# Moving the work at the seams of a two-layer kernel, and the first projection of each attention round

## The reference

```
xn = layernorm(x); s = L0_attn(xn); g = silu(L0_ffn(xn)); x = x + s * g
xn = layernorm(x); s = L1_attn(xn); g = silu(L1_ffn(xn)); x = x + s * g

L0_attn: gates f, i, o, z = xn W + b; c[t] = f c[t-1] + i z; out = o * tanh(layernorm(c))
L0_ffn:  4 trees of depth 5: each node's logits decide the child; the rows of the
         nodes on the path are gathered and summed: gelu(logits) * W_out
L1_attn: q, k, v = silu(conv4(xn W)), a gated delta rule over the 256 steps
         (16 heads of 8), out = rmsnorm(o) * silu(xn Wg) Wo
L1_ffn:  2 layers on 2 x 1024 tokens of 8 heads of 64:
         h = shift(x); q, k = rotary(l2norm(h wqkv)); x = x + softmax over a window of
         64 (own and previous block) @ wo; h = layernorm(shift(x)) * lng + lnb
         a, g = split(h w1 + b1); x = x + (a * gelu(g)) w2 + b2
```

## Time and profile before

| | |
|---|---|
| median of 3 executions | 1556.36 us (1556.31 to 1559.45) |
| the profiled execution | 1542.85 us, of it 1541.0 us span from first to last instruction |
| busy | PE 1294.8 us, DVE 1270.8, ACT 1228.2, POOL 945.8 |
| mean granted clock of TensorE | 0.938 of full |

### The profile page before, as it was taken

One profiled execution on the slowest core, in us unless ns is written; L12 is line 12 of the kernel. 1 busy time (PEld: TensorE's weight loads), 2 busy tenths in 40 slices (PEclk: granted clock), 3 DMA queues, 4 the chain that ended last, 5 costly groups with the idle time before them and its releaser, 6 DMA issues.

```text
span 1541.0 us, 31140 instructions
## 1 busy us (share of the span) xinstructions
PE 1294.8 (84%) x9368; PEld 881.3 (57%) x9368; DVE 1270.8 (82%) x4138; ACT 1228.2 (80%) x3366; POOL 945.8 (61%) x1472
## 2 busy tenths in 40 slices
PE   6987878888787665897589999999999999999986
PEld 3655656656566442343256666666666666666665
DVE  3278898978889896388499999999999999999985
ACT  2267887979787885677388998998989999989985
POOL 0237455464655641078587877878778778778752
PEclk9899999899999777898799999999999999999998
DMA  4359687696867875379301110111101111101243
GB/s 112 116 190 333 220 288 251 211 324 210 294 236 258 309 274 181 107 226 307 136 22 44 34 30 25 44 44 36 43 12 45 44 44 34 39 16 44 68 106 101
DMA packets 152407, 210.31 MB, mean 136 GB/s; under 512 B 68272, under 2 KB 105520, under 8 KB 152112
## 3 DMA queue, kind: packets, MB, share of 16 engines
q0 software_dynamic: 36864, 134.76, 25.0%
q1 hardware_dynamic: 114944, 71.98, 16.9%
q10 hardware_dynamic: 432, 1.59, 0.3%
HBM read 168.97 MB, written 26.74 MB: 127 GB/s over the span
## 4 chain that ended last, share of the span: by engine, by line
PE 26%; ACT 17%; issue 6%; DVE 2%; POOL 1%; ACTq 0%; DVEq 0%; POOLq 0%
ACT lo_s_ps L1756 5%; PE lo_qk_ps L1468 4%; PE lo_h_ps L1572 4%; PE lo_s_ps L1524 3%; PE lo_o_ps L1562 3%; ACT L1845 2%; ACT prepared_then_rounds L1816 2%; PE lo_ft_ps L1544 2%; ACT prepared_then_rounds L1770 2%; ACT lo_sq L1738 2%; PE lo_v_ps L1474 2%; PE lo_h_ps L1582 1%; PE lo_s_ps L1511 1%; ACT prepared_then_rounds L1764 1%; PE lo_o_ps L1496 1%
## 5 line engine op out<-in xcount | busy, mean ns | idle before, releaser
L341 POOL DMA_INDIRECT wide<-in_table,l_idx x128 | 129.6, 1012 | 204.2 <-DVE l_idx L810 128.7
L1756 ACT ACTIVATE lo_s_ps<-lo_s_ps,lo_nmx,lo_rn 128x128 f32<-128x128 f32 x504 | 219.5, 440 | 2.0 <-DVE lo_nmx L2073 1.6
L341 POOL DMA_INDIRECT l_rows<-in_table,l_idx x128 | 126.8, 990 | 81.9 <-DVE l_idx L817 45.7
L768 DVE CUSTOM_DVE_ANT_0 wide<-wide,xn_tok 128x128 f32<-128x128 f32 x512 | 155.9, 368 | 6.5 <-DMA wide<-in_table,l_idx 5.0
L1948 POOL TENSOR_TENSOR lo_de_kS<-lo_de_S,lo_de_ops 128x384 f32<-128x384 f32 x128 | 154.6, 1208 | 10.0
L651 ACT ACTIVATE l_rows<-l_rows,l_act 128x128 f32<-128x128 f32 x512 | 153.1, 387 | 1.0
L651 ACT ACTIVATE wide<-wide,l_act 128x128 f32<-128x128 f32 x512 | 153.1, 387 | 1.0
L768 DVE CUSTOM_DVE_ANT_0 l_rows<-l_rows,xn_tok 128x128 f32<-128x128 f32 x512 | 145.1, 347 | 7.6 <-DMA l_rows<-in_table,l_idx 7.6
L446 PE MATMUL l_S<-pre,l_AT 128*128 128x144 f32 (+3 forms) x832 | 129.3, 306 | 21.6 <-ACT l_AT L642 19.7
L446 PEld LDWEIGHTS l_S<-pre,l_AT 128*128 128x128 f32 (+2 forms) x832 | 116.2, 206 | 52.1 <-ACT l_AT L642 36.4
L1468 PE MATMUL lo_qk_ps<-wide,lo_hT 128*128 128x512 f32 x256 | 127.4, 621 | 18.6 <-DVE lo_c L2065 12.3
(11 more groups left out here) (321 smaller groups left out, 3655.0 us busy)
## 6 DMA issues: line engine op xcount, KB each, us to landing
lo_VE<-lo_V SPq DMA_DIRECT2D x64, 128.0 KB, 3.0
scratch_ops<-prepared_then_rounds SPq DMA_DIRECT2D x4, 1792.0 KB, 7.3
lo_de_ops<-scratch_ops SPq DMA_DIRECT2D x16, 448.0 KB, 4.2
scratch_qo<-prepared_then_rounds SPq DMA_DIRECT2D x8, 512.0 KB, 8.6
lo_de_qo<-scratch_qo SPq DMA_DIRECT2D x16, 256.0 KB, 4.6
x_tok<-in_x SPq DMA_DIRECT2D x8, 256.0 KB, 5.2
wide<-in_table,l_idx POOLq DMA_INDIRECT x128
l_rows<-in_table,l_idx POOLq DMA_INDIRECT x128
```

The costliest lines, as they stand in the source:

```text
L341: pool.indirect_dma_start(rows[L][:, r % SLOTS, p, :], None, a[f"table{L}"], bass.IndirectOffsetOnAxis(ap=at[:, p:p + 1], axis=0)).then_in ...
L768: ins = dve.tensor_tensor_reduce(z, z, x, 1.0, bias, ALU.mult, ALU.add, accum_out=pick[L][:, r % 2, k:k + 1])
L1756: ins = act.activation(here, here, ACT.Exp, scale=rn[:, v % 2, j, 2 * k + e:2 * k + e + 1], bias=nmx[:, j, e, k:k + 1], accum_out=sums[:, ...
```

## The change

Eight edits:

1. In `layer0_phase`, the load of the weights also waits for the last rows of level 5.
2. The bias product moves from the end of `prepare_phase` to the end of `layer0_phase`: TensorE does it ahead of `turn_m` of the last group, where it waits for the weights; VectorE's addition comes last in the phase. `b1` now lies in `wide`.
3. At the end of `prepare_phase`, the last two stores of gates and the store of the last answers are issued by ScalarE instead of SyncE.
4. The clearing of a column of `hT` moves from the start of `local_phase` to the start of `prepare_phase`.
5. In `local_phase`, TensorE waits for the constants only at its first `center`.
6. The projection of unit 0's second half goes to `s_ps` instead of `qk_ps`, so that it doesn't wait for the rotation of the first half.
7. In each round, `project(t, 0)` goes ahead of `turn_qk(t-1, 0, 0)` and `contract(t-3)`. The orders of VectorE, ScalarE and GpSimd in the rounds stay.
8. At the end, VectorE does the last unit's two products first, then those of part 7; SyncE's last stores follow, nine transfers in all instead of ten.

```diff
@@ layer0_phase, sync
             sp.wait_ge(spread[4].sem, spread[4].after(NT - 1))
+            sp.wait_ge(got[5][(NT - 1) % SLOTS].sem, got[5][(NT - 1) % SLOTS].after((NT - 1) // SLOTS))
             for k in WEIGHTS:
@@ layer0_phase, tensor
+            def bias():
+                pe.wait_ge(weights_in, 16 * len(WEIGHTS))
+                pe.wait_ge(acc_read.sem, acc_read.after(NG - 2))
+                for L_ in range(LAYERS):
+                    for side in (0, 1):
+                        for k, (at, wd) in enumerate(HCH):
+                            c, n = COLS["lnb1"] + L_, 6 * L_ + 3 * side + k
+                            ins = pe.matmul(acc[NG % 2][0:wd, 0, n:n + 1], m["w1"][:, L_, side * HID + at:side * HID + at + wd],
+                                            m["cols"][:, c:c + 1], start=True, stop=True)
+                ins.then_inc(multiplied.sem, 1)
...
+                if g == NG + 4:
+                    bias()
                 if on(g - 5):
                     turn_m(g - 5)
@@ prepare_phase, sync
-            keep(T // CT - 1)
-            for g in range(NG - 2, NG):
-                keep_gate(g)
+            keep(T // CT - 1, False)
@@ prepare_phase, scalar
+            for g in range(NG - 2, NG):
+                keep_gate(g)
+            keep_answers(T // CT - 1)
@@ local_phase
+        qk_of = lambda u, i: s_ps if (u, i) == (0, 1) else qk_ps
@@ local_phase, sync
             sp.wait_ge(last_ready.sem, last_ready.after(0))
+            sp.dma_start(rows(out)[:, NT - 2:NT, :], y_last[:, :, 3, :]).then_inc(y_stored.sem, 16)
+            sp.wait_ge(last_ready.sem, last_ready.after(1))
+            for h in (0, 1):
+                sp.dma_start(rows(out)[:, NT - 8 + h:NT - 2:2, :], y_last[:, h, 0:3, :]).then_inc(y_stored.sem, 16)
+            sp.wait_ge(last_ready.sem, last_ready.after(2))
             sp.dma_start(rows(out)[:, tiles(7), :], by_tile(u_buf(7))).then_inc(y_stored.sem, 16)
@@ local_phase, tensor
-            pe.wait_ge(consts.sem, 1)
             def project(u, i):
...
-                if n:
-                    pe.wait_ge(parts.sem, n)
+                if n >= 2:
+                    pe.wait_ge(parts.sem, n if n > 2 else 1)
...
                 if on(t - 2):
                     weigh(t - 2, 0)
+                if on(t):
+                    project(t, 0)
                 if on(t - 1):
                     turn_qk(t - 1, 0, 0)
                 if on(t - 3):
                     contract(t - 3)
-                if on(t):
-                    project(t, 0)
                 if on(t - 1):
                     turn_qk(t - 1, 0, 1)
@@ local_phase, vector, the end
             output(LAST)
-            multiply(7)
-            add_x(7)
             multiply_last(0, 3, 4)
-            add_last(0, 3, 1)
             multiply_last(3, 4, 5)
             add_last(3, 4, 2)
+            multiply(7)
+            add_last(0, 3, 2)
+            add_x(7)
```

More of the change, by code:

```diff
@@ L251, in layer0_phase @@
         scaling, scaled_rows = st("norm_scaling"), st("norm_rows")
+        multiplied = st("bias_multiplied")
         norm_rounds = [r for r in range(NG + 4) if 0 <= r < NG or 0 <= r - 4 < NG]
@@ L915, in _ @@
                     norms(g)
+            dve.wait_ge(multiplied.sem, 1)
+            for wd, ks in ((P, (0, 1)), (HCH[2][1], (2,))):
+                chunks = lambda ap: ap.rearrange("p (a k) -> p a k", k=3)[0:wd, :, ks[0]:ks[-1] + 1]
+                dve.tensor_tensor(chunks(m["b1"]), chunks(acc[NG % 2][:, 0, 0:6 * LAYERS]),
+                                  chunks(m["cols"][:, COLS["b1"]:COLS["b1"] + 6 * LAYERS]), ALU.add)
 def sized(ap):
@@ L997, in get, with keep @@
                 sp.dma_start(Y[x][:, n % 2].rearrange("p d t -> p (d t)"), scr[x][n].rearrange("b (h d) t -> (b h) (d t)", d=HD)).then_inc(y_in[x][n % 2].sem, 16)
-            def keep(c):
+            def keep(c, both=True):
                 sp.wait_ge(dve_done.sem, dve_done.after(2 * c + 1))
@@ L1004, in keep @@
                 sp.dma_start(rows, ops[:, c % 2].rearrange("p (s n) x -> p s (n x)", n=CB // 2)).then_inc(kept[c % 2].sem, 16)
-                for k, z in enumerate((qt, ow)):
+                for k, z in enumerate((qt, ow) if both else (qt,)):
                     sp.dma_start(scr["qo"][c, :, k], z[:, c % 2].rearrange("p n i g d -> p (n i g d)")).then_inc(kept[c % 2].sem, 16)
@@ L1053, in _ @@
                 pe.matmul(bank[g % 3][:], m["WgT"][:], m["xT_pad"][:, g * SG:(g + 1) * SG, TAPS - 1:], start=True, stop=True).then_inc(gated.sem, 1)
[L1054 to L1062, removed]
         @block.scalar
@@ L1107, in silu_gate, with keep_gate, keep_answers @@
                 act.activation(gate_buf[g], bank[g % 3][:], ACT.Silu).then_inc(gate_silued.sem, 1)
+            def keep_gate(g):
+                act.wait_ge(gate_silued.sem, gate_silued.after(g))
+                act.dma_start(scr["gate"][2 * g:2 * g + 2].rearrange("b r t -> r b t"), gate_buf[g].rearrange("p (b t) -> p b t", t=T)).then_inc(gate_stored.sem, 16)
+            def keep_answers(c):
+                act.wait_ge(pool_done.sem, pool_done.after(2 * c + 1))
+                act.dma_start(scr["qo"][c, :, 1], ow[:, c % 2].rearrange("p n i g d -> p (n i g d)")).then_inc(kept[c % 2].sem, 16)
             act.preload_act_table_set("natural_log_exp_and_others")
@@ L1266, in _ @@
                 dve.wait_ge(dve_done.sem, dve_done.after(n))
[L1267 to L1271, removed]
 def load_chunk(sp, m, scr, c):
@@ L1449, in _ @@
             sp.wait_ge(last_ready.sem, last_ready.after(0))
-            sp.dma_start(rows(out)[:, tiles(7), :], by_tile(u_buf(7))).then_inc(y_stored.sem, 16)
[L1451 to L1455, removed]
+            sp.dma_start(rows(out)[:, NT - 2:NT, :], y_last[:, :, 3, :]).then_inc(y_stored.sem, 16)
[3 more added lines that the diff above has]
+            sp.wait_ge(last_ready.sem, last_ready.after(2))
+            sp.dma_start(rows(out)[:, tiles(7), :], by_tile(u_buf(7))).then_inc(y_stored.sem, 16)
+            sp.wait_ge(y_stored.sem, y_stored.after(8))
         @block.tensor
         def _(pe):
-            pe.wait_ge(consts.sem, 1)
             def project(u, i):
@@ L1502, in scores @@
                 pe.wait_ge(k_kept.sem, k_kept.after(v, j + 1))
+                if (v, j) == (0, 0):
+                    pe.wait_ge(parts.sem, parts.after(0))
                 if (v, j) == (LAST, 1):
```

24 lines of the change are left out of this document (12 added, 12 removed).

## The result

The changed kernel takes 1660.01 us (median of 4 executions, 1655.09 to 1669.65), the kernel before on the same chip 1557.9: a ratio of **1.066 (1.0604 to 1.0715)**, +102 us. The forecast was +78 and the upper end of the range 1658. The direction and the mechanism were as predicted; the rounds cost 21 us more than in the sum. Of the kernels further down, one execution of turn_first took 2432 us where its other three took 1631 to 1638, and it stays out of the comparisons.

A forecast was written before the change was run, and what follows sets the result against it. Rounds, with TensorE and VectorE both over 92% busy, were taken as the bound. Stall +72.5 and clock +19, less 13.9 at the seams, gave +77.6 on 1556.36: 1634 us, range 1602 to 1658.

The forecast's parts named there:

- the mechanism: In the rounds: the contraction behind the projection makes VectorE's output 3.51 us late, delaying probabilities and TensorE's later steps.
- the size of the stall: In each round, TensorE's path from the second turn of q on runs 2.5 us late; 29 rounds make +72.5 us.
- The clock term: In the rounds, new TensorE idle time drops the clock in half of them, 1.3 us each: +19 us.
- The first rival: In the rounds: the same stall but the clock stays up, +58.6 us, 1615 us in all; chance 0.37.
- The second rival: In the rounds: projection 0.74 us earlier shortens each, 21.5 us gained, 1521 us in all; chance 0.03.
- The third: Rival: something else takes up the 3.5 us, rounds stay and only the seams count, 1542 us; chance 0.02.
- The fourth: Rival at layer 0's end: late weights make the bias product hold back the last group, 1642 us; chance 0.06.
- First layer: End of layer 0, edits 1 and 2: level 5's last rows arrive sooner, bias product fits idle time, -6.5 us.
- Preparation: End of preparation, edits 3 to 5: stores moved off SyncE give -2.1 us, first projection's wait for clearings gone -0.5.
- First unit: Edit 6: second projection in its own bank follows at once, GpSimd's wait shrinks, -3.3 us.
- The end: Edit 8: VectorE multiplies the last unit's product while waiting for the last mix, and fewer last stores, -1.5 us.

The follow-up runs named there:

- turn_first: The changed kernel with TensorE's order weigh, turn, project, contract, so only the contraction is behind the projection: ratio 1.0791, 120 us over the kernel before.
- order_only: The kernel before with edit 7 alone: ratio 1.0767, 117 us over the kernel before.
- output_late: The changed kernel with VectorE taking both answers and the first normalise ahead of output: ratio 1.0067, 10 us over the kernel before.
- contract_first: The changed kernel with TensorE's order weigh, contract, project, turn: ratio 1.0046, 6 us over the kernel before.
- scale_early: The changed kernel with GpSimd scaling k before the fourth step of the delta rule in a round: ratio 1.0637, 98 us over the kernel before.
- fill4: The changed kernel plus four unread matmuls a round in TensorE's idle time ahead of the turn of probabilities: ratio 1.0533, 80 us over the kernel before.
- seams_only: The changed kernel with edit 7 alone undone, the seven seam edits kept: ratio 0.993, 12 us under the kernel before.
- seams_early_w: The kernel with the seam edits alone, without edit 1's added wait for the weights' load: ratio 0.996, 6 us under the kernel before.

## Why the prediction was right and wrong

**The mechanism was right, and it is shown.** The changed kernel loses in the rounds alone (order_only), through VectorE's wait for the late contraction (output_late, contract_first), and the signs that the prediction named for the rounds are in the trace: the projection right behind `add_parts`, after 1.57 us of idle time (1.4 were named), 3.61 us before `output` (3 to 3.5), 2.51 us before the turn of probabilities (2.3), periods of over 26 us, clocks under 1.00 in some rounds.

**The step that failed is the size of the stall, "2.5 us late", 29 rounds times 2.5.** It is 3.06, 88.7 us instead of 72.5. Measured from `add_parts`: `output` starts 5.95 us behind it, before 2.26, so 3.69 late (3.51 in the prediction: the projection follows 0.11 us later than worked out, and the rest is in the contraction). `normalise` is 4.03 late, not 3.51 again: the square beside GpSimd takes 0.51 us more, the multiplication ahead of it 0.17 less. The turn of probabilities is then 3.53 late (2.99 in the prediction), and the second turn of q 3.08 (2.5). The prediction carried VectorE's rows over with their durations, though what ran beside them on GpSimd had moved. Without the collision the round has 25.95 us (scale_early), 2.47 over the kernel before. That this meets the predicted 2.5 so closely is partly luck: `output` is still 0.18 us later there than worked out, and the two multiplications behind it are 0.24 us shorter than in the kernel before (0.28 and 0.43 us for 0.45 and 0.50).

A smaller slip: the 671.6 us that the prediction gives to the 29 rounds are the window from 800 us on; the 29 periods take 680.97. Nothing in its sum hangs on it.

**The clock term was right in kind and nearly in size.** Half of the rounds, 1.3 us each, made 19; the trace has 16 rounds near 28 us, 1.5 us each, 24.2. fill4 confirms it as a cost. The half was a choice that no row behind it gave, and that 16 of 29 came out is luck. The first rival (the clock stays up) is out. That the term can't be worked out from the number of gaps alone shows in scale_early and turn_first: gaps of 1.93 and 2.83 us made the clock fall in 23 of 29 rounds and in all of them.

**The second rival** (the earlier projection shortens the round) is out: its own test, that `output` waits for less than 1.7 us, gives 3.61, and in contract_first, where VectorE doesn't wait, the round takes 24.10. **The third** (the rounds stay) is out. **The fourth** (weights too late) did not come: they are issued from 601.88 on, and the bias product starts at 620.11 right behind TensorE's step before it. `turn_m` has its input at 624.27 and starts at 624.69, when the product is over: 0.4 us late. The product took 4.72 us instead of 2.82, at a granted clock of 0.50 (windows from 618 to 624); in seams_only, at 0.92, it took 2.55 and left 1.92 us of idle time before `turn_m`.

**The seams**, predicted at -13.9:

- First layer, edits 1 and 2: -6.5 predicted. From the last indirect transfer to the start of the preparation it is 37.43 us, before 44.03: -6.6. Right. Seams_only and seams_early_w differ there by 6.7 us in their traces, and by 6 in their medians.
- Preparation: from its start (632.30) to that of the rounds (744.64) 112.34 us, before 114.48: -2.1, as predicted. The first projection starts 0.05 us behind GpSimd's, before 0.49: -0.4.
- First unit: -3.3 predicted. Alone (seams_only) the stretch to the first output projection is 46.65 us, before 50.06: -3.4. Together with edit 7 it is 48.63, -1.4: the projection in front costs 2 us of it in the first rounds (with edit 7 alone, order_only, the stretch is 52.75: +2.7). The prediction had priced the two edits apart.
- The end: from the last output projection of the rounds 68.12 us, before 69.39: -1.3 (-1.5 predicted).

In all -11.8 by the trace. Seams_only has -12 by its medians (6.5 to 15 by its interval), and -16 by its trace, in which the preparation (111.25) and the end (66.88) are a little shorter than above. 112.9 - 11.8 = 101.1, the medians' +102; the two profiled executions are 114 us apart, because the first layer up to its last indirect transfer happened to be 13.3 us longer in the trace of the changed kernel.

## What to carry to other kernels

When a step is moved on one engine, follow its result to the engine that takes it in order, and add the delay there, not where the step was: three steps of TensorE changed places, none got longer, and 3.7 us of VectorE's wait made each of 29 rounds 3 us longer. A moved step also moves what runs beside it: a small VectorE multiplication took twice as long beside GpSimd's, and an idle TensorE of 2 to 3 us a round cost the clock on top. A pipeline with under 2 us of slack a round leaves the gains at its seams, where each is paid once, and those were worth 12 to 19 us.

## What the runs showed of the hardware

- More work on TensorE made the kernel shorter: with four matmuls whose results nobody reads, put into an idle time of 2.51 us, 29 rounds took 23 us less and the granted clock stayed at 1.00.
- The falls of the clock are not in proportion to the idle time. With one gap of 2.51 us a round, every second round has a fall of 1.5 us; with 1.93 us, in rounds that are 0.6 us shorter, 23 of 29 have one; with 2.83 us, all. (The first two kernels have a second gap of 1.57 us; output_late, with that one and no other over 0.7 us, keeps a clock of 1.00.) A shorter gap can cost more. What decides between them was not separated further.
- A VectorE multiplication of 128x128 f32 takes 0.28 to 0.72 us in nearly all rounds, and 1.01 to 1.09 us where it meets a GpSimd multiplication of about 1 us (128x512, or 128x384 in seams_scale). GpSimd's can be held up too: the scaling of k takes 1.18 us instead of 1.04 in the changed kernel, where a VectorE multiplication starts with it, and still 1.04 in turn_first, where it starts before the square.
